# Row maxima of the first attention job taken in two halves of the queries, the second half during its scores

## What is computed

```python
scores = jnp.einsum('bhqd,bhkd->bhqk', Q, K) * scale
bias = lam[:, None, None, None] * prior_bias[None, None]
dense_out = jnp.einsum('bhqk,bhkd->bhqd', jax.nn.softmax(scores + bias, axis=-1), V)
Kg, Vg = K[:, :, idx], V[:, :, idx]
s_scores = jnp.einsum('bhsd,bhskd->bhsk', Q, Kg) * scale
sparse_out = jnp.einsum('bhsk,bhskd->bhsd', jax.nn.softmax(s_scores, axis=-1), Vg)
out = jnp.where(use_sparse[:, None, None, None], sparse_out, dense_out)
```

## Time and profile before

| | us |
|---|---|
| median of three runs | 1678.82 |
| lowest and highest | 1673.56, 1681.29 |
| the profiled execution | 1676.56 |
| its span | 1674.8 |
| first score matmul of job 0 | at 119.32 |
| PE, DVE busy over the span | 1558.6, 879.6 |
| ACT, POOL busy over the span | 726.8, 700.7 |

### The profile page before, as it was taken

The page is one execution under the profiler, slowest core; times in us unless marked ns, Lnnn a source line. Parts: engine busy times, 40 slices in busy tenths (PEclk is TensorE's granted clock), DMA queues, the critical chain, the costliest instruction groups (busy, mean ns, idle before and its releaser), DMA issues. The chain is left out here.

```text
span 1674.8 us, 20466 instructions
## 1 busy us (share of the span) xinstructions
PE 1558.6 (93%) x7344; PEld 761.4 (45%) x7392; DVE 879.6 (53%) x2048; ACT 726.8 (43%) x990; POOL 700.7 (42%) x515
## 2 busy tenths in 40 slices
PE   5789999889999999898989888999999999999998
PEld 3423333223333333433433333555656577777755
DVE  6578878889677856557755733343322111111141
ACT  4754665456566565476635566233211111111110
POOL 5437999878799999153210121400000300000070
PEclk9669999999999999999998998999999999999999
DMA  3461033232231320344432015100040005243071
GB/s 99 142 156 31 25 77 74 58 92 76 69 87 40 72 52 8 78 113 112 117 79 63 22 39 164 60 1 0 0 151 3 24 1 177 97 147 127 16 127 24
DMA packets 75905, 121.43 MB, mean 73 GB/s; under 512 B 14920, under 2 KB 53265, under 8 KB 72731
## 3 DMA queue, kind: packets, MB, share of 16 engines
q1 hardware_dynamic: 72155, 113.62, 24.2%
q0 software_dynamic: 3072, 6.03, 2.1%
q10 hardware_dynamic: 576, 0.47, 0.1%
HBM read 85.08 MB, written 36.96 MB: 73 GB/s over the span
## 5 line engine op out<-in xcount | busy, mean ns | idle before, releaser
L1140 POOL TENSOR_TENSOR sb_prob<-sb_prob,sb_weight 128x1024 f32<-128x1024 f32 x192 | 448.9, 2370 | 50.7 <-ACT sb_prob L1347 50.3
L1347 ACT ACTIVATE sb_prob<-wide 128x1024 f32<-128x1024 f32 (+3 forms) x384 | 347.8, 917 | 227.0 <-PE wide L1960 123.7
L1955 PE MATMUL wide<-sb_stack_q,sb_stack_k 99*128 99x512 bf16 (+3 forms) x896 | 281.9, 363 | 22.4 <-DVE sb_prob L1674 9.0
L1635 DVE CUSTOM_DVE_ANT_0 sb_junk<-bank,sb_bias 128x512 bf16<-128x512 f32 x340 | 227.0, 687 | 58.6 <-PE bank L1928 56.0
L1391 ACT ACTIVATE sb_sil<-wide 128x320 f32<-128x320 f32 (+1 forms) x128 | 66.2, 518 | 437.7 <-PE wide L2034 437.7
L1928 PE MATMUL bank<-sb_stack_k,sb_stack_q 96*128 96x512 bf16 (+3 forms) x598 | 216.7, 379 | 24.3 <-DVE sb_rowmax L1635 11.5
L2034 PE MATMUL wide<-sb_weight,sb_ffn 128*128 128x512 f32 x512 | 233.9, 600 | 0.0
L1975 PE MATMUL wide<-sb_prob,sb_v_aug 128*17 128x512 f32 (+3 forms) x1792 | 223.6, 566 | 8.5 <-ACT sb_o_raw L1360 7.2
L1629 DVE TENSOR_REDUCE sb_rowmax<-bank 128x1 f32<-128x512 f32 (+3 forms) x258 | 139.2, 559 | 87.1 <-PE bank L1931 55.6
L1766 DVE TENSOR_TENSOR sb_act_s<-sb_sil,wide 128x512 f32<-128x512 f32 x64 | 44.0, 687 | 256.1 <-ACT sb_sil L1391 256.1
L1178 POOL DMA_INDIRECT sb_weight<-slots_out,sb_slot_r x32 | 31.5, 986 | 285.2 <-issue 283.3
(11 more groups left out here) (270 smaller groups left out, 1836.8 us busy)
## 6 DMA issues: line engine op xcount, KB each, us to landing
sb_stack_k<-parts SPq DMA_DIRECT2D x32, 256.0 KB, 7.0
o_raw<-sb_o_raw SPq DMA_DIRECT2D x32, 256.0 KB, 2.2
sb_big<-rg SPq DMA_DIRECT2D x8, 1024.0 KB, 5.0
sb_big<-ru SPq DMA_DIRECT2D x8, 1024.0 KB, 7.2
sb_big<-rd SPq DMA_DIRECT2D x8, 1024.0 KB, 10.9
sb_stack_q<-parts SPq DMA_DIRECT2D x16, 384.0 KB, 5.1
parts<-sb_o_norm SPq DMA_DIRECT2D x40, 128.0 KB
sb_stack_q<-parts SPq DMA_DIRECT2D x16, 256.0 KB, 5.5
```

The source lines that it names most:

```text
L1140: e.tensor_tensor(p, p, weight_of(*u[1:]), ALU.mult).then_inc(weigh_p.handle, 1)
L1347: e.activation(p[:, :, first:HALF], sc[:, :, first:HALF], ACT.Exp).then_inc(SC.empty_sem(u), 1)
L1635: e.tensor_tensor_reduce(out=junk[:, i % 2, 0:hi - lo], in0=BK.tile(u)[:, 0:hi - lo], in1=bias[:, qt, lo:hi], scale=1.0, scalar=-3e38, op0 ...
L1955: i = e.matmul(sc[:, j * HALF + first:(j + 1) * HALF], stack_k[0:ROWS_M, n % 3, g, kt * P:(kt + 1) * P], stack_q[0:ROWS_M, n % 3, g, half ...
```

## The change

Job 0's maxima are split by queries: group 0 is query tiles 0 to 3, group 1 is tiles 4 to 7. `fin` and `turn` of job 0 exist once for each group, on half as many columns (PE turns 4 tiles instead of 8, ACT copies 512 columns instead of 1024, each of the four DMAs moves 3 x 512 instead of 3 x 1024). A score waits for its own half's rows only. All other jobs keep one `fin` and one `turn`.

The front list then has: 16 maxima of head 0 (all tiles, as before), the 24 of group 0 in heads 1 to 3 with a table group after every second and `("stack", 1)` after the 9th, then the six `fin` steps and the `turn` of group 0, with one maximum of group 1 after each of ten places. The 14 group 1 maxima that are left run beneath job 0's units, ahead of job 1's 64. These 78 are spread over the first 0.72 of job 0 (0.6 before); `fin` and `turn` of group 1 follow the 14; those of job 1 come 0.12 of the job later than before.

```diff
+FIRST_LEAD, BETWEEN = 0.72, 1
...
-    out = spread(mine, 0, LEAD, max_cost) if mine else []
+    lead = LEAD if n else FIRST_LEAD
+    out = spread(mine, 0, lead, max_cost) if mine and n else []
     if n + 1 < len(JOBS):
         steps = finish(n + 1) + [None] + [("turn", n + 1)]
-        out += [(LEAD + FIN_AT[k] / units_of(n), u) for k, u in enumerate(steps) if u]
-    return out + (spread(after, LEAD, 1, max_cost) if after else [])
+        out += [(lead + FIN_AT[k] / units_of(n), u) for k, u in enumerate(steps) if u]
+    return out + (spread(after, lead, 1, max_cost) if after else [])
...
-    for k, u in enumerate([u for u in steps if u[2]]):
+    for k, u in enumerate([u for u in steps if u[2] and not queries_of(0, u[3])]):
         plan.append(u)
-        if k % 4 == 0 and tables:
+        if k % 2 == 0 and tables:
             plan += tables.pop(0)
-        if k == 3 * NT:
+        if k == NT:
             plan.append(("stack", 1))
-    return plan + finish(0) + [("turn", 0)]
+    rest = [u for u in maxima(0) if u[2] and queries_of(0, u[3])]
+    for k, u in enumerate(finish(0, 0) + [None, turn(0, 0), None, None]):
+        plan += ([u] if u else []) + rest[k * BETWEEN:(k + 1) * BETWEEN]
+    return plan + [u for f in tables for u in f], rest[(k + 1) * BETWEEN:]
+
+
+def second_half(rest):
+
+    out = spread(rest + maxima(1), 0, FIRST_LEAD, max_cost)
+    at = out[len(rest)][0]
+    return out + [(at + FIN_AT[k] / units_of(0), u) for k, u in enumerate(finish(0)) ] + [
+        (at + FIN_AT[FIN_STEPS + 1] / units_of(0), turn(0))]
...
                 elif kind == "turn":
                     n = u[1]
+                    cols = slice(0, S) if n else slice(u[2] * HALF, (u[2] + 1) * HALF)
                     w.wait_ge(BK.emptied(u))
                     for h in range(QUAD):
-                        e.dma_start(stack_q[ROWS:ROWS_M, n % 3, h],
-                                    mrow[h * PARTS:(h + 1) * PARTS, 0]).then_inc(mrow_done.handle, 16)
+                        e.dma_start(stack_q[ROWS:ROWS_M, n % 3, h, cols],
+                                    mrow[h * PARTS:(h + 1) * PARTS, 0, cols]).then_inc(mrow_done.handle, 16)
...
-                    for mark in [BK.emptied(v) for v in MAXES[n][-2:]]:
+                    for mark in [BK.emptied(v) for v in MAXES[n] if queries_of(n, v[3]) == (NH - 1 if n else g[0])][-2:]:
...
-                    w.wait_ge(mrow_done.after((n, QUAD - 1)))
+                    w.wait_ge(mrow_done.after((n, QUAD - 1) if n else (n, half, QUAD - 1)))
```

More of the change, by code:

```diff
@@ L210, in max_width, with finish, fin, turn @@
     return min((half + 1) * HALF, (qt + 1) * P if JOBS[n][0] else S) - half * HALF
-def finish(n):
-    return [("fin", n, k) for k in range(FIN_STEPS)]
+def finish(n, g=NH - 1):
+    return [fin(n, k, g) for k in range(FIN_STEPS)]
+def fin(n, k, g=NH - 1):
+    return ("fin", n, k) if n else ("fin", n, k, g)
+def turn(n, g=NH - 1):
+    return ("turn", n) if n else ("turn", n, g)
+def queries_of(n, qt):
+    return NH - 1 if n else qt * NH // NT
 def mix_stages(b):
@@ L377, in attention_plan @@
     plan = []
+    first, rest = first_plan()
     extras, more = halves(projection(0, 1))
@@ L402, in attention_plan @@
             steps = [(opened + (0.9 - opened) * k / len(extras), 0, k, f) for k, f in enumerate(extras)]
-            steps += [(at, 1, k, f) for k, (at, f) in enumerate(max_stream(n))]
+            steps += [(at, 1, k, f) for k, (at, f) in enumerate(max_stream(n) + ([] if n else second_half(rest)))]
             steps = [(at, f) for at, _, _, f in sorted(steps)]
@@ L436, in attention_plan @@
     plan.append(("o", len(JOBS) - 1, 1))
-    return first_plan() + with_splits(flat(plan), SPLIT_AT)
+    return first + with_splits(flat(plan), SPLIT_AT)
 def route_plan(b):
@@ L737, in build @@
                     for k in range(3)]
-        mrow_done = signal("store_mrow", [(u[1], h) for u in of("turn") for h in range(QUAD)], 16)
+        mrow_done = signal("store_mrow", [(*u[1:], h) for u in of("turn") for h in range(QUAD)], 16)
         tab_in = [signal(f"load_tables{k}", [u for u in of("kb_load") if u[2] % 2 == k], 16) for k in range(2)]
@@ L1295, in _ @@
                 elif kind == "fin" and u[2] % 2:
-                    _, n, k = u
-                    top, rem, rem2 = (mneg[:, i] for i in range(3))
-                    part = mpart[:, n % 2, :, :, k // 2].rearrange("p n h -> p h n")
+                    _, n, k, *g = u
+                    qs = slice(0, NT) if n else slice(g[0] * NT // NH, (g[0] + 1) * NT // NH)
+                    top, rem, rem2 = (mneg[:, i, :, qs] for i in range(3))
+                    part = mpart[:, n % 2, qs, :, k // 2].rearrange("p n h -> p h n")
                     if n >= 2:
-                        w.wait_ge(BK.filled(("turn", n - 2)))
-                    w.wait_ge((rest_p if k > 1 else top_d).after(("fin", n, k - 1)))
+                        w.wait_ge(BK.filled(turn(n - 2)))
+                    w.wait_ge((rest_p if k > 1 else top_d).after(("fin", n, k - 1, *g)))
                     e.activation(part, (top, rem, rem2)[k // 2], ACT.Copy, scale=-1.0).then_inc(top_a.handle, 1)
@@ L1349, in _ @@
                     n = u[1]
+                    cols = slice(0, S) if n else slice(u[2] * HALF, (u[2] + 1) * HALF)
                     w.wait_ge(BK.filled(u))
                     if n:
-                        w.wait_ge(mrow_done.after((n - 1, QUAD - 1)))
-                    e.activation(mrow[:, 0], BK.tile(u)[0:PARTS * QUAD].bitcast(BF16),
+                        w.wait_ge(mrow_done.after((*turn(n - 1)[1:], QUAD - 1)))
+                    e.activation(mrow[:, 0, cols], BK.tile(u)[0:PARTS * QUAD].bitcast(BF16)[:, cols],
                                  ACT.Copy).then_inc(BK.empty_sem(u), 1)
@@ L1625, in _ @@
                     if n >= 2:
-                        w.wait_ge(top_d.after(("fin", n - 2, 0)))
+                        w.wait_ge(top_d.after(fin(n - 2, 0)))
                     w.wait_ge(BK.filled(u))
@@ L1933, in _ @@
                 elif kind == "turn":
-                    n = u[1]
+                    n, *g = u[1:]
                     out_rows = BK.tile(u)[0:PARTS * QUAD].bitcast(BF16)
-                    w.wait_ge(top_a.after(("fin", n, FIN_STEPS - 1)))
+                    w.wait_ge(top_a.after(("fin", n, FIN_STEPS - 1, *g)))
                     w.wait_ge(BK.vacant(u))
-                    for qt in range(NT):
+                    for qt in range(NT) if n else range(g[0] * NT // NH, (g[0] + 1) * NT // NH):
                         i = e.transpose(out_rows[:, qt * P:(qt + 1) * P],
```

18 lines of the change are left out of this document (10 added, 8 removed).

## The result

| | before | changed |
|---|---|---|
| median, 19 runs each, us | 1678.82 | 1683.08 |
| lowest and highest, us | 1671.26, 1682.21 | 1673.36, 1691.16 |
| the profiled execution, us | 1676.56 | 1673.36 |
| its span, us | 1674.8 | 1671.6 |

The ratio of the times on record is 1.0033, with a 95% interval of 1.0019 to 1.0046: 5.5 us slower, 3.2 to 7.7. It is an estimate over all runs; the plain quotient of the two medians is 1.0025, or 4.3 us. The time lies in the forecast's range, and the ratio within the 0.5% that the forecast took for no change. Neither interval holds 1, so the change costs something, and the forecast of +1.9 us was too low.

A forecast was written before the change was run, and what follows sets the result against it. It took DVE's maxima and a chain of small steps to bound the front, PE and DVE job 0's second half. Terms -4.1 + 4.0 + 0.5 + 1.5 = +1.9 us: profiled execution 1678.5, forecast 1680.7, range 1672 to 1688.

The forecast's parts named there:

- The start of the chain: Ahead of job 0: `fin` starts 3.4 us earlier, held by ACT's table groups, and the half-size turn is shorter; -4.1 us.
- no earlier start: Rival, chance 0.13: group 16's table input lands late, so job 0 starts where it did; +6.0 us, 1684.8.
- The ten maxima beneath the chain: Group 1 maxima between the steps ahead of job 0 fill idle DVE while the turn waits for ACT; no cost.
- The fourteen maxima in job 0: One in units 0 to 15, 13 in units 16 to 31, between 0.22 and 0.61 us each; +4.0 us.
- the old quarter: Quarter of job 0's second half with 12 maxima, 8.50 us, read as what DVE needs: 12 x 0.61 + 1.22.
- POOL's pace: Rival, chance 0.16: POOL bounds job 0's second half, so the 13 maxima and second turn cost nothing there; 1676.7.
- The second `fin` and turn: Within job 0: six small steps and four more transposes for group 1; +0.5 us, nothing waits.
- Job 1's turn: Moves from 5 units ahead of job 1 to 2, so PE waits at job 1's first score; +1.5 us.
- the slower rival: Chance 0.11: job 1's rows come late, 6.2 us, and the clock falls, 2.1 us lost; +8.7, 1687.4.
- the forecast's own list of signs: Wrong if first score before 110 or after 118, job 0 79.0 us or over 86, or half clock at job 1's entry.
- after job 0 all stays the same: Jobs 1 to 7 taken for unchanged: the plan as before, but for bank numbers shifted by one.

The follow-up runs named there:

- e13: The changed kernel timed a second time, unchanged; ratio to before 1.0046 (1.0029 to 1.0064).
- e3: The changed kernel with job 1's seven loads moved behind all table groups and group 0's turn; ratio to before 0.9994.
- e1: The changed kernel with the maxima spread over 0.6 of job 0 instead of 0.72; ratio to before 1.0023.
- e8: The changed kernel with no group 1 maxima beneath the chain, all 24 in job 0; ratio to before 1.0067.
- e2: The changed kernel with all 24 group 1 maxima ahead of job 0, three to a place, and spread 0.6; ratio to before 0.9988.
- e12: The changed kernel with two maxima to a place and spread 0.62, job 1's loads not moved; ratio to before 1.0023.
- e5: The kernel of before with job 1's seven loads moved behind the turn; ratio to before 1.0045.
- e7: The changed kernel with three maxima to a place, spread 0.6, and job 1's loads moved behind the last table input; ratio to before 0.9985.
- e6: The changed kernel with two maxima to a place, spread 0.62, and job 1's loads between the last table input and the turn; ratio to before 0.9955.
- e11: The changed kernel with only job 1's loads moved, between the last table input and the turn; ratio to before 1.0017.
- e10: The same kernel as e6 (two to a place, spread 0.62, loads moved), timed again; ratio to before 0.9981.
- e9: The kernel of before with job 1's seven loads moved only behind the last table; ratio to before 1.0008.

## Why the prediction was right in its class and too low in its size

*The start of the chain (-4.1 forecast): right, for the reason given.* The 14th group was to wait some 5 us for its DMA and waited 6.17; the first `fin` activation was to come 3.4 us earlier and came 4.3 (3.3 in e13); the first score 4.1 earlier, and by job 0's first exponential it was 4.4 (3.8 in e13). It wasn't the 14.6 us of maxima taken off DVE, because ACT was behind its tables, and e3 shows that without the loads 6.3 us more of it come out. Group 14 started at 98.98 rather than 102, of which 2.2 is the execution's own head start. The rival "no earlier start" is excluded: the 16th group started with no wait. But the gain isn't as firm as two traces make it look. e1 has the same front, and its first exponential came at 31.02, only 2.2 us earlier than before. Group 14 waited 7.25 us there, and the last projection ahead of the first score took 3.21 us instead of 2.04, with the granted clock at 0.57 over these us instead of 0.91:

```profile
110.40:112.30 1.90, 1.90 (x5) 0.81 (x4) 0.42 (x1) 0.00 (x0) 0.00 (x0) 0.91 0.39 64
```

```profile
113.80:116.90 3.10, 3.10 (x6) 1.20 (x5) 0.42 (x1) 0.00 (x0) 0.00 (x0) 0.57 0.65 134
```

The first row is the changed kernel, the second e1. In both the clock was at half from the maxima stage on and rose to full shortly ahead of the first score; when it does differs from one execution to the next, and moves the start of job 0 by over 1 us.

*The ten maxima beneath the chain (0): right.* e8, without them, starts its scores no earlier.

*The fourteen maxima in job 0 (+4.0): this is the term that was mis-sized.* The second half grew by 7.0 us, where +3.5 stood for its 13 maxima. With the 1.0 us of the first half and less the 0.6 of the second `fin`, 7.4 us are left for the 14; if the 0.81 us that PE waited at job 1's first score is taken off as well, 6.6. That is 0.47 to 0.53 each. (In e1, which has no such wait, it is 8.1 us or 0.58 each.) The quarters were to take 9.1, 10.1, 8.5 and 8.5. These are the old first quarter, from which the forecast had its 8.50, and the four new ones, between the exponentials of units 16, 20, 24, 28 and job 1's first (columns as in the earlier trace rows):

```profile
166.65:175.15 8.50, 8.21 (x42) 2.46 (x42) 8.46 (x25) 4.08 (x5) 7.76 (x5) 1.00 0.11 30
```

```profile
161.06:170.31 9.25, 8.57 (x44) 2.69 (x44) 9.21 (x28) 4.08 (x5) 8.64 (x5) 1.00 0.10 27
170.31:180.83 10.52, 10.01 (x47) 3.16 (x46) 8.75 (x27) 6.26 (x8) 7.47 (x4) 1.00 0.16 51
180.83:190.47 9.64, 8.46 (x43) 2.65 (x43) 9.16 (x28) 4.80 (x7) 8.62 (x7) 1.00 0.06 15
190.47:200.79 10.32, 8.96 (x51) 3.05 (x50) 8.65 (x26) 4.99 (x5) 7.58 (x4) 1.00 0.01 3
```

The first two are near the forecast; the last two, with 12 maxima each, took 1.1 and 1.8 us more. The step that failed was to take the old quarter for what 12 maxima cost. In it DVE was busy for 8.46 of 8.50 us, which is a best case. In the third new quarter DVE had 9.16 us of work, not 8.5, and 0.5 us of idle time. In the fourth it had 8.65 us of work and 1.7 us of idle time; PE's wait of 0.81 us for job 1's rows falls into it.

PE's waits point at DVE. In the old second half PE waited only once for longer than 0.1 us, for 0.34 us. In the new one it did ten times: nine waits, 2.5 us together, ended with DVE, and the tenth was the 0.81 us.

A better row to read was the share of a longer stretch: DVE was busy 41.38 of 46.2 us in the old first half, 90%. 28.1 + 13 x 0.61 = 36.0, and 36.0 / 0.9 = 40.0 us; the stretch took 39.73 with DVE at 35.77, 90%. That is worked out afterwards, and the 90% is an average over quarters with different limits: DVE was at 100%, 83%, 95% and 84% in the four above, and in the second one PE was busy for 10.01 of 10.52 us. Other numbers of maxima come out alike:

| run | maxima of job 0 within job 0 | job 0 | DVE busy in it | rest |
|---|---|---|---|---|
| before | 0 | 79.00 | 69.47 | 9.5 |
| e2 | 0 | 79.63 | 69.56 | 10.1 |
| e12 | 4 | 82.79 | 72.05 | 10.7 |
| changed | 14 | 87.04 | 77.81 | 9.2 |
| e8 | 24 | 94.63 | 84.22 | 10.4 |

The job is as long as DVE's work in it and 9.2 to 10.7 us more, in each of these. Between neighbouring rows from e2 on a maximum cost 0.8, 0.4 and 0.8 us, so the 0.62 is a mean. It doesn't hold where something else stops the job: in e5, with its wait of 8.81 us, the rest is 20.6. PE, at 97% of the old second half, looked like the bound there; in the new one it is at 91%.

*POOL's pace (the rival of 1676.7, and the nearest to what the Trainium skill's "Perfetto Trace Analysis", section "Identifying the Most-Contended Engine" would make of POOL's 92% in the old second half): fallen.* Work added on DVE lengthened the job while POOL went down to 32.31 of 39.73, 81%. A busy share ranks the engines of a stretch as it is; which of them sets the length was shown here only by adding work to one.

*The second `fin` and turn (+0.5): right.* e2 and e7, which have no other addition in job 0, are 0.6 us longer than before.

*Job 1's turn (+1.5): right in kind, half as large.* PE waited 0.81 us at job 1's first score; e1, e2 and e12, where that turn stands earlier, have no such wait. No stretch of lower clock followed there, so the slower rival's mechanism didn't come: the measured 5.5 us lie about midway between the forecast's 1.9 and its 8.7, by another cause than either.

*The sum.* Forecast at job 1: -4.1 + 4.0 + 0.5 + 1.5 = +1.9. Seen at job 1: -4.4 + 8.0 = +3.6 (e13: -3.8 + 8.0 = +4.3). The 8.0 is 6.6 for the maxima, 0.6 for the second `fin` and turn, and 0.8 for job 1's turn. The interval of the times, 3.2 to 7.7, holds both. Jobs 1 to 3 took 202.1 us against 203.1 before, so nothing more was lost there in these executions. Whether the rest up to the measured 5.5 lies anywhere but in the scatter is open; one candidate, job 7, is told of below.

That the time lies in the range is weak evidence for the sum: 1672 to 1688 is wide enough to hold no change at all, and the forecast's own list of signs called it wrong if job 0 was longer than 86 us. It was 87.04.

## What to carry to other kernels

An unbroken run of work at the highest pace that a profile shows is a best case, and not the price of a dozen additions in a row. In this kernel it was nearer to take the busy share that the loaded engine reached over a longer stretch (90% on DVE) and divide the new busy time by it. That is a rule of thumb fitted to one job of one kernel. Before a stage is shortened, list what else ends beneath it: a wait of 7 us that cost nothing beneath DVE's work became the next bound, and its cause, seven loads standing ahead of three small ones on a queue, was worth more than the edit (e3, e6). When such loads are moved, they must not be issued just ahead of the next small transfers that something waits for (e11), nor so late that their own readers wait (e5).

## What was not expected

*Behind the same idle gap of PE the granted clock falls in one execution and not in the next.* e6 and e10 are one kernel. In job 7 PE waited 3.07 us for DVE in both. In e6 the score behind the gap took 0.39 us, and the stretch of 10 us around it was granted the full clock:

```profile
647.39 0.39 PE L1988 MATMUL wide<-sb_stack_q,sb_stack_k 99*128 99x512 bf16 x1 [3.07 <-DVE sb_prob L1707]
```

```profile
640.00:650.00 10.00, 6.88 (x43) 2.33 (x47) 4.22 (x7) 4.57 (x7) 10.00 (x7) 1.00 0.07 27
```

In e10 it took 0.61, and the clock of the stretch that lies the same way about the gap was 0.81 in the mean:

```profile
645.88 0.61 PE L1988 MATMUL wide<-sb_stack_q,sb_stack_k 99*128 99x512 bf16 x1 [3.07 <-DVE sb_prob L1707]
```

```profile
638.49:648.49 10.00, 6.88 (x36) 2.32 (x37) 3.32 (x6) 3.79 (x5) 9.62 (x6) 0.81 0.07 27
```

Job 7, from its first exponential to job 8's, took 59.7 us in e6 and 62.5 in e10. The row with this gap of 3.03 to 3.08 us is in all 14 profiled executions. In six of them (before, e1, e2, e5, e6, e9) the score behind it took 0.39 us and job 7 took 59.7 to 59.8. In seven (both of the changed kernel, e3, e7, e10, e11, e12) it took 0.61 and job 7 took 62.5 to 62.8. e8 lies between: the score took 0.39 us, the granted clock fell to 0.51 over 664.7 to 668.0, 1.4 us behind the score's start, and job 7 took 61.4. A difference of 3 us between two single traces may be this alone, and has to be looked for here before an edit is credited with it.

This touches the forecast that after job 0 all stays the same. All three executions with the order of before fall on the fast side, and only three of the eleven others. If the changed order did meet the lower clock there more often, that would be worth up to 3 us, and could hold the 1.9 us that the sum at job 1 leaves of the measured 5.5. But e6 and e10 show that the order doesn't decide it, one profile for each kernel can't give a frequency, and adding it to the marks at job 1 doesn't bring them nearer to the ratios for all kernels (e11: 4.3 + 2.7 us against 2.9 measured). It stays open.
